# Group sums of a graph attention layer: loads, stores and vectors on other queues, one maximum and one reciprocal for two units

## The reference

```python
logits = jnp.einsum('ehd,ehd->eh', q[src], k[dst])
a = logits + dist_attn + path_attn
mx = jax.ops.segment_max(a, dst, num_segments=N)
e = jnp.exp(a - mx[dst])
s = jax.ops.segment_sum(e, dst, num_segments=N)
sa = e / s[dst]
msg = v[src] * sa[:, :, None]
agg = jax.ops.segment_sum(msg, dst, num_segments=N).reshape(N, D)
x = agg @ Wo + bo
```

## Time and profile before

| what | value |
|---|---|
| runs shown | 818.81, 819.82, 812.48 us (median 818.81) |
| the profiled execution | 812.19 us |
| its span, first to last instruction | 810.2 us |
| busy: PE, DVE, ACT, POOL | 696.5, 532.6, 417.8, 121.8 us |
| mean granted TensorE clock | 0.944 |
| attention block, from the barrier before it to the one behind it | 96.3 to 313.6 us of the span |

### The profile page before, as it was taken

The page is one execution under the profiler, slowest core; times in us unless marked ns, Lnnn a source line. Parts: engine busy times, 40 slices in busy tenths (PEclk is TensorE's granted clock), DMA queues, the critical chain, the costliest instruction groups (busy, mean ns, idle before and its releaser), DMA issues. The chain is left out here.

```text
span 810.2 us, 14580 instructions
## 1 busy us (share of the span) xinstructions
PE 696.5 (86%) x4978; PEld 547.9 (68%) x4978; DVE 532.6 (66%) x1162; ACT 417.8 (52%) x689; POOL 121.8 (15%) x187
## 2 busy tenths in 40 slices
PE   3988755787879765999999999999999999999994
PEld 2654333454546442599999679968889899887793
DVE  6737594897989531644322654358878888888855
ACT  5235332675767651754333643237767666676640
POOL 7341264242420021000000001300000000000022
PEclk9999886898989976999999999999999999999997
DMA  9734395657565764300002040966767677766114
GB/s 250 193 60 92 77 140 140 201 151 215 170 195 188 235 182 145 128 1 1 1 1 79 0 156 26 377 202 218 247 206 226 235 237 241 259 224 230 64 58 152
DMA packets 104156, 125.62 MB, mean 155 GB/s; under 512 B 32402, under 2 KB 70060, under 8 KB 103564
## 3 DMA queue, kind: packets, MB, share of 16 engines
q1 hardware_dynamic: 96955, 115.06, 45.8%
q0 software_dynamic: 5600, 6.54, 3.5%
q10 hardware_dynamic: 1520, 3.01, 1.8%
HBM read 94.91 MB, written 29.67 MB: 154 GB/s over the span
## 5 line engine op out<-in xcount | busy, mean ns | idle before, releaser
L2220 PE MATMUL ps<-xT,w_hi 128*128 128x480 f32 (+7 forms) x512 | 110.5, 338 | 2.2 <-DVE hT L2039 2.2
L2220 PEld LDWEIGHTS ps<-xT,w_hi 128*128 128x128 f32 x512 | 82.1, 189 | 9.4 <-DVE hT L2039 4.0
L2025 DVE TENSOR_TENSOR w_lo<-weights_far,w_hi 128x1024 fp32r<-128x1024 f32 x64 | 78.0, 1219 | 2.5 <-ACT w_hi L2135 2.2
L2222 PEld LDWEIGHTS ps<-xT,w_lo 128*128 128x128 f32 x512 | 73.5, 190 | 1.5
L2222 PE MATMUL ps<-xT,w_lo 128*128 128x240 f32 (+7 forms) x512 | 74.5, 268 | 0.0
L193 POOL DMA_DIRECT2D windows<-window_scratch x104 | 59.7, 577 | 93.0 <-DVE onehot L990 76.2
L1113 PE MATMUL ps<-onehot,group_weights 128*32 128x314 bf16 x1272 | 59.7, 331 | 15.8 <-DVE onehot L990 8.2
L2135 ACT ACTIVATE w_hi<-weights_far 128x1024 fp32r<-128x1024 f32 x64 | 67.1, 1051 | 0.0
L990 DVE TENSOR_SCALAR onehot<-iota_h,windows 128x628 bf16<-128x628 f16 x212 | 66.8, 378 | 0.0
L2245 PE MATMUL ps<-w_hi,hidden 128*128 128x512 f32 (+3 forms) x176 | 62.2, 405 | 2.7 <-DVE hidden L2049 1.9
L1135 PE MATMUL ps<-ident,weights 126*128 126x126 f32 (+1 forms) x200 | 34.0, 308 | 32.2 <-ACT weights L1072 22.6
(11 more groups left out here) (309 smaller groups left out, 1530.4 us busy)
## 6 DMA issues: line engine op xcount, KB each, us to landing
weights_far<-in_L_ffn_w SPq DMA_DIRECT2D x64, 512.0 KB, 5.6
sums_scratch<-sums_out SPq DMA_DIRECT2D x53, 314.0 KB, 3.3
weights_near<-in_L_ffn_w SPq DMA_DIRECT2D x32, 512.0 KB, 3.5
sums_in<-sums_scratch SPq DMA_DIRECT2D x40, 309.1 KB
weights_near<-in_L_gnn_W SPq DMA_DIRECT2D x4, 1024.0 KB, 13.3
weights_near<-in_L_ffn_sw SPq DMA_DIRECT2D x8, 512.0 KB, 5.0
weights_near<-in_L_gnn_Wqkv SPq DMA_DIRECT2D x3, 1024.0 KB, 8.2
weights_ff<-in_L_gnn_W SPq DMA_DIRECT2D x1, 3072.0 KB, 13.0
```

What stands on the lines that cost most here:

```text
L2025: dve.tensor_tensor(to[1], raw_rest[n] if v == V else raw[u][n], to[0], ALU.subtract)\
L2220: pe.matmul(both(bank, cap), w[u % 2][0][:, c, cut], xT(r)[:, c, :, :], start=c == 0, stop=False)
L2222: last = pe.matmul(bank[:, 0:cap], w[u % 2][1][:, c, cut], xT(r)[:, c, 0, :], start=False, stop=c == DC - 1)
```

## The change

Four things are changed, all of them in or around the attention block.

1. **Who loads windows.** POOL takes one block in four (w % 4 = 3), SP the other three. LOADED is 5: `projections` loads blocks 0, 1, 2 and 4, all by SP, and POOL loads block 3 in the attention block. SP reads the offsets of its three blocks at once (12 values), POOL four at a time. SP loads all of its blocks up to 17 before it asks for the rows of pair 0; after that it loads block w + 6 just ahead of the store of block w.
2. **Who stores.** ACT issues the stores of the 14 leading blocks itself, each behind its copy; SP stores the rest.
3. **Rows and small DVE steps by pairs.** One DMA brings the sums of both units of a pair (two buffers of twice the size); one `tensor_reduce` gives both guards, one reciprocal both inverses; ACT takes over `collect`, ahead of the next pair's two `norm`.
4. **The vectors** are loaded by ACT at the start of the attention block and no longer by SP at its end.

The core of the diff:

```diff
-LOADED = 6
+LOADED = 5
+POOLS = 3
...
 def by_pool(w):
-    return w % 4 >= 2
-def place_at(w):
...
-def load_starts(nc, engine, w, tab):
-    n = min(2 * GW, GROUPS - GW * w)
+    return w % (POOLS + 1) == POOLS
+def load_starts(nc, engine, w, blocks, tab):
+    n = min(blocks * GW, GROUPS - GW * w)
     _, starts = nc.values_load_multi_w_load_instructions(tab[0:1, REL + GW * w:REL + GW * w + n], engines=[engine], min_val=0,
                                                          max_val=CHUNK * REC2)
...
-        frm = region[bass.ds(starts[GW * (w % 2) + j], P * REC2)] if k else region[0:P * REC2]
+        frm = region[bass.ds(starts[j], P * REC2)] if k else region[0:P * REC2]
...
             for w in range(LOADED):
                 if not by_pool(w):
-                    starts = load_starts(nc, mybir.EngineType.SP, w, tab) if w % 2 == 0 else starts
-                    load_groups(sp, w, starts, rec2_d, windows, g_in)
+                    if w % (POOLS + 1) == 0:
+                        starts = load_starts(nc, mybir.EngineType.SP, w, min(POOLS, LOADED - w), tab)
+                    load_groups(sp, w, starts[w % (POOLS + 1) * GW:], rec2_d, windows, g_in)
...
-            pool.wait_ge(ends_ready, 1)
-            pool.wait_ge(windows_stored, 16)
-            for w in range(LOADED):
-                if by_pool(w):
-                    starts = load_starts(nc, mybir.EngineType.Pool, w, tab) if w % 2 == 0 else starts
-                    load_groups(pool, w, starts, rec2_d, windows, g_in)
...
-        sums_in = [sb(f"sums_in{i}", [P, SRC]) for i in range(4)]
+        sums_in = [sb(f"sums_in{i}", [P, 2 * SRC]) for i in range(2)]
...
+    both = banks.rearrange("p (b a) n -> p b a n", a=2)[:, 0:2, :, 0:SH]
...
-            starts = None
-            def block(w):
-                nonlocal starts
-                nxt = place_at(w)[1]
-                if w % 2 == 0 and nxt < WB:
-                    starts = load_starts(nc, mybir.EngineType.SP, nxt, tab) if nxt % 2 == 0 else starts
-                    wait_past(sp, windows_stored, stored_for(nxt))
-                    window_free(sp, nxt)
-                    load_groups(sp, nxt, starts, rec2_d, windows, g_in)
+            starts, first = None, None
+            def load(w):
+                nonlocal starts, first
+                if w < WB and not by_pool(w):
+                    if w % (POOLS + 1) == 0 or starts is None:
+                        starts, first = load_starts(nc, mybir.EngineType.SP, w, POOLS - w % (POOLS + 1), tab), w
+                    wait_past(sp, windows_stored, stored_for(w))
+                    window_free(sp, w)
+                    load_groups(sp, w, starts[(w - first) * GW:], rec2_d, windows, g_in)
+            def stored(w):
                 sp.wait_ge(w_copied, w + 1)
                 sp.dma_start(sums_d[w, :, :], sums_out[w % 3]).then_inc(out_done[w % 3], 16)
-            def unit_rows(u):
-                tile, h = divmod(u, H)
+            def pair_rows(q):
+                tile, h = divmod(2 * q, H)
                 if h == 0:
                     for i in range(3):
                         sp.wait_ge(out_done[i], 16 * len(range(i, window_blocks(tile), 3)))
-                wait_past(sp, summed, u - 3)
+                wait_past(sp, summed, 2 * q - 2)
                 g0 = tile * TILE // GD
-                rows = sums_d.rearrange("w (j d h) n -> (w j) d h n", j=GW, h=H)
-                sp.dma_start(sums_in[u % 4][0:TILE, :], rows[g0:g0 + TILE // GD, 0:GD, h, :]).then_inc(units_in[u % 4], 16)
-            for w in range(window_blocks(0) + 1):
-                block(w)
-            unit_rows(0)
-            unit_rows(1)
-            for w in range(window_blocks(0) + 1, leading):
-                block(w)
+                rows = sums_d.rearrange("w (j d h) n -> (w j) d (h n)", j=GW, h=H)
+                sp.dma_start(sums_in[q % 2][0:TILE, :], rows[g0:g0 + TILE // GD, 0:GD, h * SRC:(h + 2) * SRC])\
+                  .then_inc(units_in[q % 2], 16)
+            for w in range(LOADED, window_blocks(0) + 7):
+                load(w)
+            pair_rows(0)
+            for w in range(window_blocks(0) + 7, leading + AHEAD):
+                load(w)
             for q in range(PAIRS):
                 if q + 1 < PAIRS:
                     assert blocks_by(q) >= window_blocks((2 * q + 2) // H)
-                    unit_rows(2 * q + 2)
-                    unit_rows(2 * q + 3)
+                    pair_rows(q + 1)
                 for w in pair_blocks(q):
-                    block(w)
+                    load(w + AHEAD)
+                    stored(w)
                 if PAIRS - 5 <= q < PAIRS - 1:
                     load_w1(sp, W1, w_near, [q - PAIRS + 5], w1_in)
         sp.wait_ge(windows_stored, 16 * len(ROUNDS))
-        for i, vec in enumerate((bo, b2)):
-            sp.dma_start(rows_b[:, i * D:(i + 1) * D], vec.rearrange("(a n) -> a n", a=1).broadcast_to([P, D]))\
-              .then_inc(ff_vec_in, 16)
-        sp.dma_start(rows_c[0:MC, :], b1.rearrange("(m p) -> m p", p=P)).then_inc(ff_vec_in, 16)
-        for i, vec in enumerate((ln2_g, ln2_b)):
-            sp.dma_start(rows_c[MC + i * DC:MC + (i + 1) * DC, :], vec.rearrange("(m p) -> m p", p=P))\
-              .then_inc(ff_vec_in, 16)
...
-            starts = None
-            for w in range(WB):
-                nxt = place_at(w)[0]
-                if w % 2 == 0 and nxt < WB and nxt % 2 == 0:
-                    starts = load_starts(nc, mybir.EngineType.Pool, nxt, tab)
-                if w % 2 == 0 and nxt < WB:
-                    wait_past(pool, windows_stored, stored_for(nxt))
-                    window_free(pool, nxt)
-                    load_groups(pool, nxt, starts, rec2_d, windows, g_in)
+            for w in range(POOLS, WB, POOLS + 1):
+                starts = load_starts(nc, mybir.EngineType.Pool, w, 1, tab)
+                wait_past(pool, windows_stored, stored_for(w))
+                window_free(pool, w)
+                load_groups(pool, w, starts, rec2_d, windows, g_in)
...
-            def guards(u):
+            def guards(q):
+                dve.wait_ge(s_ready, q + 1)
+                wait_past(dve, e_ready, 2 * q)
+                dve.tensor_reduce(small[0:TILE, 1:3], both[0:TILE], AX.XY, ALU.max, negate=True).then_inc(g_ready, 1)
...
+                dve.wait_ge(units_in[u // 2 % 2], 16 * (u // 4 + 1))
...
+                dve.tensor_tensor_reduce(PR[k][0:TILE], sums_in[u // 2 % 2][0:TILE, k * SRC:(k + 1) * SRC], L[k][0:TILE], 1.0, 1e-37, ALU.mult, ALU.add,
...
-                dve.wait_ge(summed, u + 1)
-                dve.reciprocal(inv[k][0:TILE], total[k][0:TILE]).then_inc(inv_ready, 1)
-            def collect(q):
-                tile, c = divmod(q, DC)
-                dve.wait_ge(o_ready, q + 1)
-                dve.tensor_copy(hT[:, c, tile * TILE:(tile + 1) * TILE], psO).then_inc(o_moved, 1)
+            def inverses(q):
+                dve.wait_ge(summed, 2 * q + 2)
+                dve.reciprocal(small[0:TILE, 5:7], small[0:TILE, 3:5]).then_inc(inv_ready, 1)
...
-                if w in (1, 2):
-                    guards(w - 1)
+                if w == 1:
+                    guards(0)
...
                 weights(2 * q)
-                if q:
-                    collect(q - 1)
                 weights(2 * q + 1)
                 for w in ws[0:1]:
                     masks(w)
+                inverses(q)
                 if q + 1 < PAIRS:
-                    guards(2 * q + 2)
-                for w in ws[0:1]:
+                    guards(q + 1)
+                for w in ws:
+                    if w > ws[0]:
+                        masks(w)
                     products(w)
                     onehots(w)
...
+        for i, vec in enumerate((bo, b2)):
+            act.dma_start(rows_b[:, i * D:(i + 1) * D], vec.rearrange("(a n) -> a n", a=1).broadcast_to([P, D]))\
+               .then_inc(ff_vec_in, 16)
+        act.dma_start(rows_c[0:MC, :], b1.rearrange("(m p) -> m p", p=P)).then_inc(ff_vec_in, 16)
+        for i, vec in enumerate((ln2_g, ln2_b)):
+            act.dma_start(rows_c[MC + i * DC:MC + (i + 1) * DC, :], vec.rearrange("(m p) -> m p", p=P))\
+               .then_inc(ff_vec_in, 16)
...
                 act.activation(halves(sums_out[w % 3]), psW(w), ACT.Copy).then_inc(w_copied, 1)
+                if w < leading:
+                    act.wait_ge(w_copied, w + 1)
+                    act.dma_start(sums_d[w, :, :], sums_out[w % 3]).then_inc(out_done[w % 3], 16)
...
+                act.wait_ge(g_ready, u // 2 + 1)
...
+                act.wait_ge(inv_ready, u // 2 + 1)
...
+            def collect(q):
+                tile, c = divmod(q, DC)
+                act.wait_ge(o_ready, q + 1)
+                act.activation(hT[:, c, tile * TILE:(tile + 1) * TILE], psO, ACT.Copy).then_inc(o_moved, 1)
...
                 ws = list(pair_blocks(q))
+                if q:
+                    collect(q - 1)
```

(1 more changed line is left out.)

25 lines of the change are left out of this document (1 added, 24 removed).

## The result

| | before | after |
|---|---|---|
| median of the timed runs, us | 819.32 (4 runs, 812.48 to 821.06) | 831.24 (4 runs, 826.32 to 832.25) |
| the profiled execution, us | 812.19 | 826.32 |
| its span, us, and granted clock | 810.2, 0.944 | 824.7, 0.938 |

The changed kernel is slower: the ratio, taken over all fast runs of both (a fifth run of the changed kernel took 834.59 us) and so not quite that of the two medians above, is 1.016, with a 95% interval of 1.0094 to 1.0226. In the profiled executions the attention block ends at 329.9 instead of 313.6 us. The first view is again the windows of that block: start and end, length, then busy time and instructions of PE, PEld, DVE, ACT and POOL, granted clock, DMA share and GB/s. The last line is the gap in front of the barrier.

A forecast was written before the change was run, and what follows sets the result against it. The prediction took SP's stream of offset reads and issues as the bound: 11.5 + 1.5 + 1 - 9.5 = +4.5 us, 812.2 to 816.7 profiled. As the profiled execution was near the lowest run, it forecast 823, range 805 to 835.

The forecast's parts named there:

- Leading blocks: Attention up to pair 0: SP's ten block loads and three offset reads make pair 0 start at 143.9, +5.6 us.
- Pairs 0 to 12: SP's stream between these row loads: 107.9 us of work plus 5 of waits; pair 12's rows land +13.0 us later.
- While SP is the bound: Attention pairs: DVE's and ACT's savings are worth nothing until SP has loaded block 52.
- DVE and ACT in a pair: Merged steps save DVE 0.45 us a pair; pairs 12 to 14 take 8.0 + 6.4 + 7.3, leaving +11.5 at pair 15.
- Tail: Last pairs: the first unit waits for both units' rows and sums, +1.5 us (bounds -0.5 and +3).
- Vectors and barrier: End of attention: early vectors let the barrier close behind the last mover, -9.5 us; POOL's additions cost DVE 1 us.
- fourth rival: End of attention: POOL's drain or something else at line 280 takes its 9.5 us anywhere; +14, 833 us; chance 8%.
- The lock: Pairs 10 to 12: POOL's additions lock DVE out, five times 2.8 us, 9 on the path; +13, 832 us; chance 15%.
- SP is not the bound: Attention block: offset reads and issues cost others nothing, DVE sets the pace, pair 15 at 236; near 783 us; chance 7%.
- one price, not one per value: SP's offset reads: 12 values cost the 3.3 us of eight, SP falls to about the present pace; 813 us; chance 13%.

The follow-up runs named there:

- d: Changed kernel with SP and POOL reading no window offsets in attention, windows loaded from constant places (other edges' sums), run once: 798.9 us.
- b: Changed kernel with windows split as before, POOL issuing two of four blocks, offsets read eight at a time: 815.92 us, ratio 1.003 to the kernel before.
- e: Changed kernel with the row load of pair q+2 issued during pair q, before that pair's last store: 826.72 us, ratio 1.0148 to the kernel before.
- f: Kernel b with the edit of e, so windows evenly split and row loads early: 801.8 us, ratio 0.9858 to the kernel before.
- c: Changed kernel with SP's offset read moved earlier, into the slot of POOL's block, ahead of a copy wait: 822.76 us, ratio 1.0111 to the kernel before.
- h: Kernel before with only the merged steps: one maximum and one reciprocal a pair, ACT moving the results: 816.8 us, ratio 1.0037.
- g: Kernel before with only the vectors' part: ACT loads all five vectors at the start of the attention block: 807.91 us, ratio 0.9904.
- k: Kernel before with row loads of pair q+2 issued at the head of pair q, unless they start a tile: 811.23 us, ratio 0.9954.
- a: Changed kernel with POOL's five additions moved to behind its load of block 7: 831.26 us, ratio 1.0238 to the kernel before.
- i: Kernel f with POOL's additions moved to behind its load of block 15: 804.35 us, ratio 0.9825 to the kernel before.

## Why the prediction was right in its mechanism and short in one term

**Sign and place.** The forecast was slower by 4.5 us in the profiled execution; it is 14.1. The median of 831.24 lies inside the range of 805 to 835 and 8 us above the forecast. SP is the bound, as I had said, and rows 5 priced it rightly in kind: one TENSOR_LOAD and then a step for every value. Kernel d is the direct evidence.

**Leading blocks** held: SP's issues without a pause from 103.9, its first row load at 139.9 for 138.5, pair 0 at 144.8 for 143.9. There is luck in that: ten blocks and three reads took 36.0 us where I had 33.4, and it came out because SP's first issue was 1.2 us earlier than I had put it and the rows landed 0.5 sooner.

**Pairs 0 to 12** is the step that failed, by its size. I had 107.9 us of work and 5 of waits from the row load of pair 0 to that of pair 12; it took 124.7. From SP's timeline: eight reads 38.3 us instead of 34.4; issues, with the steps between them, 79.0 instead of 73.5; waits 7.4 by the pauses in it (8.1 in the view of waits) instead of 5. That makes 3.9 + 5.5 + 2.4 = 11.8. Each term was taken from a clean instance or a median: the window load from one at 2.05 us with the step behind it, while the issues at 163.87 alone took 2.64 and others 3.13; a read from a TENSOR_LOAD of 1.04 us, while these took 1.28 in the median and up to 2.09. A stream with no slack gets the mean of its parts. The 5 us either way that I gave this sum were too little for its 138 issues and eight reads. Why a TENSOR_LOAD or an issue takes longer at some places than at others, no run shows.

**What stood behind it.** "While SP is the bound" hid a second question, what comes next. I had it only as waits for copies. Kernels b, e and f show that the chain from copy to row load is nearly as long: relieve SP alone and it takes over, shorten it alone and SP still rules. Kernel c shows that my sum also depends on where the waits stand: the same instructions in a better order took 6.7 us less.

**DVE and ACT in a pair.** Once SP's loads end I gave pairs 12 to 14 21.7 us; they took 25.9. The saving of 0.45 us a pair didn't show there. Kernel h, where the merge stands alone, is slower by 0.4%. The largest single part is pair 12, which took 10.9 us for my 8.0. In it DVE stands 2.1 us ahead of the second unit. The profile names no releaser, but the unit starts when ACT has just made its exponentials (to 273.07), and these stand in ACT's stream behind the copy of a block:

```profile
271.69 0.69 ACT L1035 ACTIVATE sums_out<-ps 128x628 f32<-128x628 f32 x1 [1.01 <-PE ps L1098]
272.29 0.78 ACT L1044 ACTIVATE exponents<-ps,small 126x628 f32<-126x628 f32 x1
...
273.19 0.81 DVE L988 CUSTOM_DVE_ANT_0 weights<-sums_in,exponents 126x628 f32<-126x628 f32 x1 [2.12 <-issue]
```

The other part is pair 14, 8.5 us for 7.3, at the end of which DVE waits 4.0 us for the rows of pair 15, after 2.8 before; SP, done with its loads, waits for the copies that stand ahead of them.

**Tail.** -3.2 us for a forecast of +1.5. The bound that I gave below nothing, that longer rows move faster, is a small part at most: from p(15) to p(19) the kernels with one row load for a pair took 23 to 26 us, those with two (before, g, h, k) 25 to 28, and within each group the time goes roughly with TensorE's granted clock. The lines are from p(15) to p(19), in the kernel before, the changed kernel and kernel a (the clock is the third number from the end):

```profile
266.96:294.24 27.28, 19.61 (x165) 14.12 (x167) 14.71 (x37) 17.77 (x25) 0.00 (x0) 0.87 0.87 245
...
296.15:319.76 23.61, 14.91 (x134) 10.03 (x132) 12.84 (x25) 17.63 (x28) 0.00 (x0) 1.00 0.87 285
...
293.58:319.85 26.27, 18.99 (x132) 12.99 (x132) 12.84 (x25) 16.75 (x26) 0.00 (x0) 0.81 0.80 257
```

Kernel a has the changed kernel's instructions in this stretch, and takes 2.7 us longer at 0.81 of full speed than that does at 1.00; c, at 0.80, took 26.2. At the clock of the kernel before, 0.87, kernel i with its one row load took 26.4, against 27.3 before and 26.3 in k, so the longer rows may be worth some 1 us or nothing. Most of the tail's gain in the profiled execution goes with the clock that it happened to be granted. That is luck: I had no term for it, and it covers 4.7 us of the 16.8 by which the stretches from pair 0 to pair 15 came out longer than forecast. What set the clock, no run shows.

**Vectors and barrier.** -9.6 for -9.5. The fourth rival (the gap stays) is out: kernel g shows the barrier's wait going from 10.9 to 1.3 us with nothing else changed. The drain did prove to be long wherever it stood (9.9 us from 257.4 in the changed kernel, 14.2 from 237.2 in g), and it is harmless far from the end.

**The lock** was right as a mechanism and wrong in both sizes: an addition takes 1.25 us, not 2.8, so the price is 6.1 us and not 14, and in the changed kernel at most 0.8 of it reach p(12) and none is measurable in the time (a). The 2.8 counted POOL's drain as part of the additions. In g 4.6 us of it are on the path, in i, where pair 0 comes 6.8 later, about all of it; in f a wait for rows would have taken its place. The Trainium skill, "SBUF — State Buffer", section "SBUF: two separate sides", is borne out by this: the one-hots stood still for the additions, while before, DVE's `hT` copy from `ps` took its usual 0.29 us in the midst of them.

**First and second rival.** "SP is not the bound" (783, where its own terms add up to 781) and "one price, not one per value" (813) fall with the register steps above and with d.

## What to carry to other kernels

A queue that issues for everybody has a stream like an engine's: add up all its instructions, with the register work that no view counts as busy, and price them at their mean under load, not at one clean instance. When it is the bound, ask what stands right behind it in length; here an edit worth 1.3% and one worth nothing measurable took 3% off together. The order within the stream counts too: reads put where it would wait anyway cost less (c). Large elementwise work on POOL belongs where DVE is waiting anyway; beside one-hots in SBUF it stops DVE for as long as it lasts, in whichever stretch it is put, and whether the time reaches the end depends on what DVE would have waited for next. And before a gain or loss of a few us in one profiled stretch is put down to an edit, its granted clock has to be compared.

## What the hardware showed that was not expected

- POOL's additions of 128x512 f32 took 1.25 us each and held DVE's one-hots (f16 to bf16, in SBUF) for 6.1 of their 6.15 us; in g and i four one-hots took 8.13 and 7.69 us beside them.
- POOL's drain at the end of a block outlasts its last shown operation: its additions end at 262.9 and the drain at 267.3 in the changed kernel; before, they end at 305.5 and the drain at 313.4. In a and i, with no addition just ahead of it, it took 6.4 and 8.0 us.
- The TENSOR_LOAD of an offset read took 0.31 to 2.09 us in one kernel, by 1.13 in the median. Each value behind it took 0.25 us on SP, and none of it is shown as busy. On POOL the TENSOR_LOAD took 0.33 us in the median.
- The same stretch of attention, pairs 15 to 19, took 23.6 us at a granted clock of 1.00 and 26.3 at 0.81 (the changed kernel and a).
